# Graph network on one Trainium2 core: fewer layer-2 tiles beside the last chunk's first four layer-1 tiles, and 46 in place of 37 split tiles

## What is computed

```python
h = maximum(layernorm(x), 0)
g = h @ W0 + B0
mask = (adj < 0.5) & ~eye
S = where(mask, exp(-(1/adj - 1/mu)**2 / (2*sigma**2)), 0)
x = x + S @ g                        # layer 1
h = maximum(layernorm(x), 0) @ W1.T
x = x + (adj*adj + eye) @ h          # layer 2
```

## Time and profile before

| | |
|---|---|
| median of 3 runs | 1899.3 us (1899.1 to 1899.39) |
| the profiled execution | 1898.44 us |
| its span, first to last instruction | 1896.6 us |
| TensorE matmul busy | 1845.0 us |
| VectorE busy | 1723.8 us |
| ScalarE busy | 1732.0 us |
| 256 layer-1 tiles and 256 layer-2 tiles, of these split | 37 |

### The profile page before, as it was taken

The page is one execution under the profiler, slowest core; times in us unless marked ns, Lnnn a source line. Parts: engine busy times, 40 slices in busy tenths (PEclk is TensorE's granted clock), DMA queues, the critical chain, the costliest instruction groups (busy, mean ns, idle before and its releaser), DMA issues.

```text
span 1896.6 us, 13279 instructions
## 1 busy us (share of the span) xinstructions
PE 1845.0 (97%) x4820; PEld 883.9 (47%) x4820; DVE 1723.8 (91%) x1011; ACT 1732.0 (91%) x986; POOL 87.3 (5%) x111
## 2 busy tenths in 40 slices
PE   6999998999999999999999999999999999999997
PEld 4544443444444444444444444444444445555564
DVE  7999999998999999999999999999999955678685
ACT  7999999899999999999999999999999997777562
POOL 0000000000000000000000000000000000000011
PEclk9999999999999999999999999999999999999999
DMA  7576877897878787777776786666666578767896
GB/s 273 196 283 258 319 290 262 273 327 267 325 238 322 244 309 275 260 244 269 257 255 241 258 299 227 244 233 227 216 225 218 194 262 280 259 234 272 311 352 196
DMA packets 82849, 497.59 MB, mean 262 GB/s; under 512 B 9568, under 2 KB 9952, under 8 KB 26592
## 3 DMA queue, kind: packets, MB, share of 16 engines
q1 hardware_dynamic: 68544, 468.94, 64.7%
q0 software_dynamic: 14240, 27.79, 8.8%
HBM read 468.91 MB, written 27.79 MB: 262 GB/s over the span
## 4 chain that ended last, share of the span: by engine, by line
PE 35%; ACT 30%; DVE 24%; issue 9%; DMA 1%; POOL 0%; DVEq 0%; POOLq 0%; SPq 0%; ACTq 0%
PE p_x L450 11%; ACT rings L747 10%; ACT rings L752 9%; DVE rings L591 9%; ACT rings L757 8%; DVE rings L584 8%; PE p_l1b L416 8%; PE p_l1a L416 6%; PE p_own L450 5%; DVE rings L602 5%; ACT rings L765 2%; DVE xa_buf L689 1%; PE p_x L428 1%; PE p_x L430 1%; PE p_x L429 1%
## 5 line engine op out<-in xcount | busy, mean ns | idle before, releaser
L591 DVE SCALAR_TENSOR_TENSOR rings<-rings,small 128x2048 f32<-128x2048 f32 x256 | 601.0, 2347 | 27.1 <-ACT rings L752 26.9
L584 DVE SCALAR_TENSOR_TENSOR rings<-rings 128x2048 f32<-128x2048 f32 x256 | 585.8, 2288 | 8.3 <-PE p_l1b L416 7.7
L757 ACT ACTIVATE rings<-rings,small 128x2048 f32<-128x2048 f32 x256 | 533.5, 2084 | 42.1 <-DVE rings L591 41.7
L747 ACT ACTIVATE rings<-rings,small 128x2048 f32<-128x2048 f32 x256 | 510.0, 1992 | 12.8 <-DVE rings L584 9.4
L450 PE MATMUL p_x<-rings,h 128*128 128x512 f32 x1128 | 512.2, 599 | 8.7 <-DVE xa_buf L689 8.7
L752 ACT ACTIVATE rings<-rings 128x2048 f32<-128x2048 f32 x256 | 488.4, 1908 | 5.5
L416 PE MATMUL p_l1b<-rings,h 128*128 128x512 f32 x1024 | 459.5, 595 | 0.0
L416 PE MATMUL p_l1a<-rings,h 128*128 128x512 f32 x1024 | 458.7, 594 | 0.0
L450 PEld LDWEIGHTS p_x<-rings,h 128*128 128x128 f32 x1128 | 215.5, 192 | 274.3 <-issue 262.8
L602 DVE TENSOR_TENSOR rings<-rings 128x2048 f32<-128x2048 f32 x135 | 308.9, 2288 | 7.4 <-DMA rings<-adjT 4.2
L416 PEld LDWEIGHTS p_l1b<-rings,h 128*128 128x128 f32 x1024 | 195.3, 191 | 243.3 <-issue 240.8
(11 more groups left out here) (89 smaller groups left out, 497.0 us busy)
## 6 DMA issues: line engine op xcount, KB each, us to landing
rings<-adjT SPq DMA_DIRECT2D x439, 1024.0 KB, 6.9
outT<-xa_buf POOLq DMA_DIRECT2D x90, 256.0 KB, 6.4
x_buf<-xT SPq DMA_DIRECT2D x32, 256.0 KB, 5.8
outT<-y_buf POOLq DMA_DIRECT2D x15, 256.0 KB, 4.5
outT<-x_buf POOLq DMA_DIRECT2D x1, 256.0 KB, 4.7
w<-W SPq DMA_DIRECT2D x1, 64.0 KB, 7.3
w<-W1T SPq DMA_DIRECT2D x1, 64.0 KB, 7.1
bias_rows<-B SPq DMA_DIRECT2D x1, 64.0 KB, 8.7
```

The lines of the kernel that those rows point to most:

```text
L584: dve.scalar_tensor_tensor(out=tile(s_ring, slot_of(t)), in0=tile(a_ring, slot), scalar=CUTOFF, in1=tile(a_ring, slot), op0=ALU.is_lt, op1 ...
L591: dve.scalar_tensor_tensor(out=v, in0=v, scalar=neg_2c, in1=v, op0=ALU.add, op1=ALU.mult).then_inc(squared, 1)
L747: act.activation(v, v, ACT.Ln, bias=tiny_c).then_inc(ln_done, 1)
L757: act.activation(v, v, ACT.Exp, bias=exp_bias, scale=neg_k).then_inc(sens_done, 1)
```

## The change

The 8 items of the last chunk's first four steps come two to a step (`FEW`, `FEW_STEPS`); the other 48 are spread evenly over the remaining twelve, four to a step. Before, all 56 were spread evenly over the 16 steps, 3 and 4 in turn. The three tail items and all that follows keep their steps. The rule of `SPLITS` becomes m % 3 != 0, two tiles in three.

```diff
--- before.py
+++ after.py
@@ -45,6 +45,7 @@
 SPLIT_ORDER = list(SPLIT_STEP)
 EVAC = 3
 STEAL = 0.5
+FEW, FEW_STEPS = 2, 4
 
 
 class Chain:
@@ -68,7 +69,9 @@
         n = QUOTA[c]
         return [(2 * k + 1) * NC // (2 * n) for k in range(n)]
     n = NC * NC - 2 * NC + 1 - sum(QUOTA) - TAIL
-    return [(2 * k + 1) * NC // (2 * n) for k in range(n)] + [NC + k for k in range(TAIL)]
+    n -= FEW * FEW_STEPS
+    return ([i for i in range(FEW_STEPS) for _ in range(FEW)]
+            + [FEW_STEPS + (2 * k + 1) * (NC - FEW_STEPS) // (2 * n) for k in range(n)] + [NC + k for k in range(TAIL)])
 
 
 def next_chain(c, places, done):
@@ -160,7 +163,7 @@
 
 
 SPLITS = [it for it in ITEMS if it.step >= LAST + SPLIT_STEP.get(it.source, STEPS) and it.row != it.source
-          and it.m % 5 % 2 == 0]
+          and it.m % 3 != 0]
 for it in ITEMS:
     it.split = None
 for r, it in enumerate(SPLITS):
```

## The result

The changed kernel takes **1905.18 us** (median of 9 runs, 1903.03 to 1907.67), the kernel before in the same comparison 1899.56 (9 runs, 1898.2 to 1901.14). The ratio is **1.0029, interval 1.0021 to 1.0038**: slower, by 5.6 us, and 0.7 us above the upper end of the forecast range. The profiled execution took 1903.03 us (span 1901.2, before 1896.6).

The account below looks back on a forecast made before the run. The prediction took TensorE to bound the last chunk, with 8.4 us of waits for VectorE's queue. Its terms summed to +0.9 us on the median of 1899.3, giving 1900.2 us, range 1893 to 1904.5.

Parts of the forecast that it names:

- 1 nine splits: Last chunk: 46 split tiles for 37, each saving TensorE 0.7 us; -6.3 us.
- 2 thin start: First four steps of the last chunk: ScalarE and VectorE stay covered by TensorE's work, nothing is late; 0.
- 3 gap at (3, 11): Steps 4 to 9: the last split of step 6 waits behind an eviction in VectorE's queue; +1.2 us.
- 4 steps 11 to 16: From (7, 13) to (1, 13): VectorE's queue, with waits for ScalarE, takes longer than TensorE's tiles; +5.5 us.
- 5 gap at (1, 14): End of layer 1: (1, 14), split instead of (0, 14), has its parts behind the relu; +1.9 us.
- 6 last tiles: End of the chunk: pair (12, 15), (13, 14) split before the diagonal squares, so both late gaps go; -1.4 us.
- The first rival: Steps 11 to 16: ScalarE's waits overlap with VectorE's queue, gaps stay near 5.0 us; 1894.7 us, chance 0.2.
- the loads: Last tiles: DMA loads at 363 GB/s become the bound, priced at 4.5 us; 1904.7 us, chance 0.13.
- VectorE as the bound of the whole chunk: Last chunk: each added split costs its 3.5 us in full, 31 us; 1930 us, chance 0.03.

Follow-up runs that it names:

- e7: Changed kernel with tile (1, 13) left whole and four extra VectorE casts ahead of the parts of (1, 12); 1904.89 us (one run).
- e4: Changed kernel with tile (1, 13) left whole, 45 split tiles; 1897.09 us, ratio 0.9982 to the kernel before.
- e6: Changed kernel with VectorE doing split parts before item squares and (0, 14) split in place of (1, 14); 1896.98 us, ratio 0.9982 to before.
- e3: Changed kernel with VectorE doing the parts of the tile ahead before the item's own square; 1898.66 us, ratio 0.9992 to before.
- e5: Changed kernel with tile (0, 14) split in place of (1, 14), 46 split tiles; 1903.41 us (one run).
- e9: Changed kernel with parts before squares and 41 split tiles listed by place in VectorE's queue; 1887.28 us, ratio 0.9937 to before.
- e2: Kernel before, with its even spread of items, given the new split rule (43 split tiles); 1905.29 us, ratio 1.0026 to before.

## Why the prediction was wrong

The forecast was 1900.2, no measurable difference, with a range to 1904.5; it came out slower, at 1905.18. By its own steps, as changes of the stretch. Measured is the time between the same two tiles in both kernels, less the tiles in between at 3.43 and 2.73 us:

| step | forecast us | measured us |
|---|---|---|
| 1 nine splits | -6.3 | -6.3 |
| 2 thin start | 0 | 0 |
| 3 gap at (3, 11) | +1.2 | +1.0 |
| 4 steps 11 to 16 | +5.5 | +6.0 |
| the clock behind the gap at (1, 13) | none | +1.6 |
| 5 gap at (1, 14) | +1.9 | +2.2 |
| 6 last tiles | -1.4 | +0.8 |
| sum | +0.9 | +5.3, as the stretch itself |

- **Terms 1 to 4 were right.** For term 4, from the end of (7, 13) at 1674.04 to the start of (1, 13) the trace has 94.56 us against 94.2 in the sum. Less the 83.5 us of its tiles that is 11.1 us of gaps (10.5 forecast), 5.5 of it at (1, 13) (about 5). The single waits of VectorE agree too (13.3 us for 13.5), so this is not two errors that cancel. The first rival, that these steps absorb the splits, is refuted.
- **A term was missing: the clock behind that gap, +1.6.** I priced a gap at its own length, and that step failed: TensorE also ran for a while at the 1.2 GHz level behind it. The trace of before shows this in chunks that I had not looked at. Its timeline of TensorE, far ahead of the last chunk:

```profile
304.07 5.40 PE L450 MATMUL p_x<-rings,h 128*128 128x512 f32 x8 [4.76 <-DVE xa_buf L689]
```

  Behind a wait of 4.76 us a plain tile took 5.40 us, where the earlier trace rows has 3.59. The granted clock of that kernel was at the lower level in six stretches of 3.41 or 6.83 us ahead of 561 us, and then not until 1891.5, which is why every stretch that I read said 1.00. In e7 a gap of about the same size as that at (1, 13), at another tile, brought a fall; in e4, without the gap, there was none.
- **Term 5 was undersized**, because it stopped an instruction too early. By its own count the relu starts 7.2 us and the parts of (1, 14) are done 11.9 us behind the last layer-1 tile; the trace has 7.2 and 12.0. But (1, 14) opens a chain, and its bank is emptied by an eviction that stands behind the parts: another 0.6 us. The gap became 2.6 us by the starts for the 1.9 of the term, and cost the stretch 2.2, which e6 gives back.
- **Term 6 failed, with the wrong sign**, off by 2.2 us, the largest error of the sum. "Both 1869.49-to-1883.18 gaps go": one did not, it became one of 2.5 us by the starts, 2.2 in the sum where before it was 1.4 for the two. I asked whether the pair (12, 15), (13, 14) would be split ahead of the diagonal squares, and did not ask what stands ahead of (14, 15): the square of (15, 15), which waits 3.16 us for its load. I took it as an operation with a duration and left its own wait out. e3 takes it out of the way, and the gap is gone. e5 shows what else I left out: I expected a gain of 2.6 us and got 0.4, because what came sooner waited 0.4 us longer behind this load, and a fall of the clock behind that wait cost 1.4.

So VectorE's queue as the cause was right, and in steps 11 to 16 its price too. Wrong were the clock, which the sum did not have, the wait in term 6, the releaser in term 5 and 0.5 us in term 4, all in the same direction. The median of the changed kernel lies a further 2.2 us above its profiled run, which is the lowest of its nine. Its three runs of mean clock 0.986 took 1907.2 to 1907.7, those of 0.990 and 0.991 1903.0 to 1905.6, which fits longer or more falls in some executions; one at 0.987 took 1903.1, which does not. No trace of those runs was read, so this stays an argument.

The rivals: **the loads** had the right time, 1904.7, by a reason that is only partly right. The queues moved 431 GB/s in the stretch ahead of (1, 13), so 363 was no ceiling, and (1, 13) and (14, 15) waited for VectorE's parts. The rule that I weighed against this rival (the Trainium skill, "Perfetto Trace Analysis", Roofline, about 435 GB/s for the 16 DMA engines) agrees with the 431. e9, which wants its tiles sooner than any other, has no gap over 0.9 us among the last. But one load, that of (15, 15), did hold up the end, through VectorE's queue. **VectorE as the bound of the whole chunk** is refuted: the change cost 5.6 us and not 31, and e6 gives VectorE the same nine splits more and is 3.6 us faster than before. With it falls, for this kernel, the reading by the highest occupancy (the Trainium skill, "Perfetto Trace Analysis", Identifying the Most-Contended Engine): weight loads are at 47% in e9 and TensorE has no more than 1.4 us of gaps in the stretch.

## What to carry to other kernels

An in-order queue gives each added piece of work the price of its place: nine more splits cost 5.6 us by a rule of counting, the same number gained 3.6 with the parts in a better order and one split moved, and four more in places that the trace picked came out 12.6 us ahead. So walk the queue from a wait whose end is known to the instruction that the bound engine needs, and give every instruction ahead of it not its duration but the time at which its inputs are there, loads above all. Ask for every semaphore that this instruction waits for: the parts of (1, 14) were on time, the eviction behind them was not. And an idle gap of TensorE can cost more than its length: look at the granted clock behind gaps of that size in other parts of the trace, even where the stretch in question is at full clock now.

## What the runs showed of the hardware

- A gap of 5.2 to 5.5 us in the stretch was followed by a time at the 1.2 GHz level each time (the changed kernel, e2, e5, e7), for 3.41 or 6.83 us, which cost 1.6 to 2.2 us. In all twelve traces every wait of TensorE of 3.08 us or more after the first 60 us had a fall with it, at least three in each.
- Behind shorter waits a fall came in some places and not in others, at the same tile too: at (1, 14), behind 2.01 us, in e2 and e7, and not in the changed kernel, e3 and e4; at (14, 15), behind 2.37 us, in e5 and not in e4 (2.34). At (1, 13) it came behind 2.59 us (e3) and 2.62 (e6), and at (2, 11) it did not come behind 2.72 to 2.76 us in six kernels. So the length of the wait alone does not decide it; what does is open.
- The DMA queues moved 431 GB/s in the changed kernel (1755 to 1765), 422 to 428 in e3 and e7; in the last chunk of before the highest that I had read was 377 (1820 to 1840).
